# Attention scores with queries and keys as two fp16 parts on 64 rows, two heads side by side

## What is computed

```python
Q = proj(Wq, bq); K = proj(Wk, bk); V = proj(Wv, bv)        # (32, 2048, 16)
query_norms = jnp.linalg.norm(Q, axis=2)
_, top_idx = jax.lax.top_k(query_norms, top_u)              # top_u = 2048 // 5 = 409
Q_sel = jnp.take_along_axis(Q, top_idx[:, :, None], axis=1)
scores = jnp.einsum('bud,bld->bul', Q_sel, K) * scale
attn = jax.nn.softmax(scores, axis=-1)
out_sel = jnp.einsum('bul,bld->bud', attn, V)
out_full = jnp.zeros((BH, L, hd), dtype=x.dtype)
out_full = out_full.at[jnp.arange(BH)[:, None], top_idx].set(out_sel)
```

## Time and profile before

| | us |
|---|---|
| runs, median of 3 | 1194.58 (1193.07 to 1196.31) |
| profiled execution, its span | 1193.6 |
| PE busy | 993.4 (83%) |
| DVE busy | 904.4 (76%) |
| ACT busy | 646.3 (54%) |
| POOL busy | 713.0 (60%) |

### The profile page before, as it was taken

One profiled execution on the slowest core, in us unless ns is written; L12 is line 12 of the kernel. 1 busy time (PEld: TensorE's weight loads), 2 busy tenths in 40 slices (PEclk: granted clock), 3 DMA queues, 4 the chain that ended last, 5 costly groups with the idle time before them and its releaser, 6 DMA issues. The chain is left out here.

```text
span 1193.6 us, 29414 instructions
## 1 busy us (share of the span) xinstructions
PE 993.4 (83%) x7725; PEld 611.1 (51%) x7726; DVE 904.4 (76%) x2197; ACT 646.3 (54%) x1448; POOL 713.0 (60%) x840
## 2 busy tenths in 40 slices
PE   7999101399999999999977873299999999999995
PEld 4444000233333333333324662287778888888894
DVE  4895588778888888888866887667778777777774
ACT  2777185157777777777763441355454444444441
POOL 1687482447888888888659992124445544554443
PEclk9999655569999999999997895599999999999998
DMA  6244772201111111111306991399982322322332
GB/s 229 105 143 164 234 243 79 59 19 44 39 47 34 46 34 46 34 46 34 84 21 205 259 272 41 77 235 226 218 204 50 50 43 48 53 44 44 53 45 27
DMA packets 129229, 118.70 MB, mean 99 GB/s; under 512 B 18128, under 2 KB 117136, under 8 KB 129168
## 3 DMA queue, kind: packets, MB, share of 16 engines
q1 hardware_dynamic: 106904, 95.02, 27.0%
q0 software_dynamic: 20480, 21.53, 11.1%
q10 hardware_dynamic: 1784, 1.44, 0.4%
HBM read 57.27 MB, written 37.60 MB: 79 GB/s over the span
## 5 line engine op out<-in xcount | busy, mean ns | idle before, releaser
L994 DVE TENSOR_REDUCE attend_mxh<-attend_p_a 128x1 f32<-128x512 f32 x416 | 264.1, 685 | 56.9 <-PE attend_p_a L1137 52.0
L1076 ACT ACTIVATE w<-attend_p_b 128x409 f32<-128x409 f32 x480 | 228.8, 514 | 95.1 <-PE attend_p_b L1153 89.3
L1875 ACT ACTIVATE expert_hr<-expert_p,b1t 128x256 f32<-128x256 f32 (+1 forms) x376 | 134.3, 423 | 194.1 <-PE expert_p L1813 174.1
L1768 POOL DMA_INDIRECT out_x<-expert_ys,expert_drop x72 | 121.2, 1684 | 193.6 <-DVE expert_ys L1910 138.2
L1153 PE MATMUL attend_p_b<-attend_qt,w 98*128 98x409 bf16 x480 | 164.4, 347 | 0.3 <-ACT w L1076 0.3
L1137 PE MATMUL attend_p_a<-w,attend_qt 96*128 96x512 bf16 x384 | 151.0, 397 | 1.8 <-DVE attend_mxh L994 0.9
L1835 PE MATMUL expert_p<-w,expert_hhi 128*128 x800 | 136.7, 273 | 0.5 <-DVE expert_ys L1910 0.2
L1813 PE MATMUL expert_p<-expert_xhi,w 128*128 128x256 f16 x800 | 136.3, 273 | 0.0
L1758 POOL DMA_INDIRECT expert_xs<-h_d,expert_take x72 | 73.0, 1014 | 75.4 <-DVE expert_take L1914 54.4
L906 POOL DMA_INDIRECT attend_qsel<-q_d,idx x96 | 92.9, 967 | 39.8 <-POOL attend_idle L934 19.4
L1163 PE MATMUL attend_p_o<-w,attend_vh 128*32 128x409 f32 x1024 | 115.2, 522 | 1.1 <-ACT w L1076 0.6
(11 more groups left out here) (355 smaller groups left out, 1984.4 us busy)
## 6 DMA issues: line engine op xcount, KB each, us to landing
expert_wu<-w SPq DMA_DIRECT2D x88, 256.0 KB
w<-in_L_ffn_w SPq DMA_DIRECT2D x20, 512.0 KB, 4.5
q_d<-project_q SPq DMA_DIRECT2D x32, 256.0 KB, 3.1
w<-k_d SPq DMA_DIRECT2D x32, 192.0 KB
k_d<-project_k SPq DMA_DIRECT2D x45, 128.0 KB
x<-in_L_attn_x SPq DMA_DIRECT2D x8, 512.0 KB
attn_d<-zero SPq DMA_DIRECT2D x8, 512.0 KB
w<-k_d SPq DMA_DIRECT2D x32, 128.0 KB
```

Source lines behind the costliest of these rows:

```text
L994: dve.tensor_reduce(mxh[:, c, k:k + 1], chunk_bank(a)[:, :], AX, ALU.max).then_inc(a_done, 1)
L1076: act.activation(prob[:, j, :], tile_bank(j)[:, 0:TOP], ACT.Exp, scale=SCALE).then_inc(prob_done, 1)
L1768: pool.indirect_dma_start(out=out, out_offset=bass.IndirectOffsetOnAxis(ap=drop[u][:, s:s + 1], axis=0), in_=ys[u][:, s, :], in_offset=Non ...
L1875: last = act.activation(hr[g % 2][:, f, rows], p_1[g][:, f, rows], ACT.Relu, bias=cst["b1t"][:, bass.ds(e[s] * FB + 2 * g + f, 1)], scale= ...
```

## The change

Q and K become two fp16 parts each, scaled by 16. A score takes three products of parts: on 64 rows per head lie K high, K low, a gap of 16 rows, and K high again against Q high, Q high, the gap and Q low. In the gap the keys hold the constant 256, and the queries hold zeros for the chunks and minus the maximum / 256 in two parts for the tiles. Two heads then fill the 128 rows: head 2p on rows 0 to 63, head 2p+1 on rows 64 to 127, each product addressed to its half of PE (`tile_position=(64 * h, 0)`). So the unit of the block is a pair of heads, of which there are 16, all written out.

- Chunks and tiles of the two heads stand next to each other on PE; their number per head, 13 and 16, and their widths are as before. Chunks now have four banks, tiles three; the bank that held `p_m` is gone.
- The maximum is folded into the queries on PE: `turn_m` turns the queries a second time and adds the maximum in PSUM (24 products a pair), and ACT copies the whole. `turn_max` and its two-row copy are gone.
- `values` takes two tiles of two heads at a time, `results` gives both heads in one product of 34 columns, `minus_maximum` and `finish` treat both heads in one go.
- POOL's idle memsets are gone; gathers and scatters wait for DVE's count of maxima, two maxima a step. `vh` has two buffers of a pair, gathered queries three.
- Keys load by two DMAs of 32 and 16 rows per head. [...]
- In `project_block` the third parts go (POOL and ACT), and the last keys take one step of DVE instead of three steps.
- In `route_block` seven scatters are left over instead of four, and SP waits for them at tile 12.

```diff
-TERMS = 6
-PARTS = 3
+PARTS = 2
 HELD = 4
-STACK_K = ((0, 3), (3, 2), (5, 1))
-KR = TERMS * HD
+ROWS_H = HELD * HD
+UNIT = 16.0
...
-                        pool.tensor_tensor(krest[oc][:, :], yk[oc][:, :], k3[j % 2][oc][:, 0, :], ALU.subtract).then_inc(krest_done, 1)
-                def third_k(j):
-                    for oc in range(KD if j < NB - 1 else 0):
-                        pool.wait_ge(kpart1_done, KD * j + oc + 1)
-                        pool.tensor_tensor(k3[j % 2][oc][:, 2, :], krest[oc][:, :], k3[j % 2][oc][:, 1, :], ALU.subtract).then_inc(kpart2_done, 1)
-                unrolled([None, None, None, None, None, second, third, last_of_block(second_k), None, last_of_block(third_k)])
+                        pool.tensor_tensor(k3[j % 2][oc][:, 1, :], yk[oc][:, :], k3[j % 2][oc][:, 0, :], ALU.subtract).then_inc(kpart1_done, 1)
...
+                    j = NB - 1
                     dve.wait_ge(k_ps, KD * NB)
-                    dve.wait_ge(krest_done, KD * (NB - 1))
-                    dve.tensor_scalar(yk[1][:, :], p_k[1][:, :], bkb[:, 1, B - 1:B], None, ALU.add).then_inc(last_y[1], 1)
...
+                        dve.scalar_tensor_tensor(out=k3[j % 2][oc][:, 1, :], in0=p_k[oc][:, :], scalar=bkb[:, oc, B - 1:B], in1=k3[j % 2][oc][:, 0, :],
+                                                 op0=ALU.add, op1=ALU.subtract).then_inc(last_second, 1)
...
+        p_a = [ps(f"p_a{i}", [P, 512], F32) for i in range(4)]
...
+        def chunk_use(q, a, h):
+            return 1 + USES_A * q + 2 * a + h + (1 if a >= TURN_AT else 0)
...
+        def tile_use(p, j, h):
+            return 1 + USES_B * p + 2 * j + h + (1 if j == TPB - 1 else 0)
...
+            q, at = divmod(before - 1, USES_A)
+            if at < 2 * TURN_AT:
+                pe.wait_ge(a_done, CHP * q + at + 1)
+            elif at > 2 * TURN_AT:
+                pe.wait_ge(a_done, CHP * q + at)
...
+                def load_rows(p, h):
+                    sp.dma_start(kt[p % KB][HP * h:HP * h + 32, :], io["k3_d"][2 * p + h].rearrange("r d l -> (r d) l")).then_inc(k_here[p % KB], 16)
+                def load_again(p, h):
+                    sp.dma_start(kt[p % KB][HP * h + 48:HP * h + 64, :], io["k3_d"][2 * p + h, 0]).then_inc(k_here[p % KB], 16)
...
+                    if p + QB < NP:
+                        pool.wait_ge(mq_ps, p + 1)
+                        for i in range(2 * FULL):
+                            turn(p, at)
+                            gather_chunk(p + QB, i)
+                            at += 1
+                    if 1 <= p and p + 1 < NP:
+                        spread_v(p + 1)
+                    if p % 2 and (p + 3) // 2 < GN:
+                        turn(p, at)
+                        gather_tails((p + 3) // 2)
+                        at += 1
+                    if p > 0:
+                        pool.wait_ge(out_done, p)
+                        for i in range(2 * FULL):
+                            turn(p, at)
+                            scatter_chunk(p - 1, i)
+                            at += 1
+                    if p % 2 == 0 and p > 0:
+                        turn(p, at)
...
+                    dve.tensor_reduce(mxh[:, h, c, k:k + 1], p_a[chunk_use(q, a, h) % 4][:, :], AX, ALU.max).then_inc(a_done, 1)
...
+                for p in range(KB):
+                    for h in range(2):
+                        dve.memset(kt[p][HP * h + 32:HP * h + 64, :], STEP_M).then_inc(fill_done, 1)
+                    if p == 0:
+                        dve.memset(mxh[:, :, :, :], -3e38).then_inc(zero_done, 1)
+                        dve.memset(mpart[:, :, :, :], 0.0).then_inc(zero_done, 1)
+                for u in range(2):
+                    dve.memset(vh[u][:, :, :, W1:VC], 0.0)
+                    dve.memset(vh[u][:, :, :, HD], 1.0)
...
+                    maxima(p + 1, 3)
+                    if p > 0:
+                        finish(p - 1)
+                    for a in range(4, NA):
+                        maxima(p + 1, a)
+                    if p + 1 < NP:
+                        minus_maximum(p + 1)
+                    for a in range(3):
+                        maxima(p + 2, a)
+                    if p == NP - 1:
+                        for i in range(EARLY):
+                            split_weight(i)
...
+                def turned(q, into, low):
+                    last = None
+                    for c in range(QT):
+                        cols = slice(c * P, min((c + 1) * P, TOP))
+                        for h in range(2):
+                            n = 2 * q + h
+                            tail = slice(32 * (n % GH), 32 * (n % GH) + QTAIL)
+                            for r in range(2):
+                                w = 2 * h + r
+                                source = qsel[q % QB][:, h, c, 32 * r:32 * r + 32] if c < FULL else qtail[n // GH % 2][:, 32 * r:32 * r + 32]
+                                last = pe.matmul(into[32 * w:32 * w + 32, cols], source, cst["identb"][:, :] if c < FULL else cst["identb"][:, tail],
+                                                 start=True, stop=not (low and r), tile_position=(0, 32 * w))
+                                if low and r:
+                                    k = P if c < FULL else QTAIL
+                                    last = pe.matmul(into[32 * w:32 * w + 32, cols], mpart[0:k, h, c, :], cst["identb"][0:k, 0:k],
+                                                     start=False, stop=True, tile_position=(0, 32 * w))
+                    return last
...
+                        use = chunk_use(q, a, h)
+                        wait_chunk_bank(pe, use)
+                        into, rows = p_a[use % 4], slice(HP * h, HP * h + HP)
+                        if c < FULL:
+                            last = pe.matmul(into[:, :], qa[q % 2][rows, c * P:(c + 1) * P], kt[q % KB][rows, k * CH:(k + 1) * CH], start=True, stop=True, tile_position=(HP * h, 0))
+                        else:
...
+                        use = tile_use(p, j, h)
+                        wait_tile_bank(pe, use)
+                        rows = slice(HP * h, HP * h + HP)
+                        pe.matmul(p_b[use % 3][:, 0:TOP], kt[p % KB][rows, j * P:(j + 1) * P], qb[p % 2][rows, 0:TOP],
+                                  start=True, stop=True, tile_position=(HP * h, 0)).then_inc(b_ps, 1)
...
+                            w, j = 2 * h + i, 2 * b + i
+                            last = pe.matmul(p_o[32 * w:32 * w + VC, 0:TOP], vh[p % 2][:, j, h, :], prob[:, 2 * (j % (TPB // 2)) + h, :],
+                                             start=(b == 0), stop=(b == BLOCKS - 1), tile_position=(0, 32 * w))
...
+                for p in range(NP):
+                    scores_tile(p, 0)
+                    if p > 0:
+                        values(p - 1, 7)
+                    scores_tile(p, 1)
+                    scores_chunk(p + 1, 3)
+                    scores_tile(p, 2)
+                    if p > 0:
+                        results(p - 1)
+                    scores_tile(p, 3)
+                    scores_chunk(p + 1, 4)
+                    scores_chunk(p + 1, 5)
+                    scores_tile(p, 4)
+                    values(p, 0)
+                    scores_chunk(p + 1, 6)
+                    scores_tile(p, 5)
+                    values(p, 1)
+                    scores_tile(p, 6)
+                    scores_chunk(p + 1, 7)
+                    values(p, 2)
+                    scores_tile(p, 7)
+                    scores_chunk(p + 1, 8)
+                    turn_q(p + 2)
...
-                LATE = 8
+                LATE = 12
 
                 def load(t, c):
                     wait(sp, at_ps, t - 3)
-                    if isinstance(t, int) and t == LATE:
-                        sp.wait_ge(scattered, 16 * QT)
+                    if t == LATE if isinstance(t, int) else c == LATE % 4:
+                        sp.wait_ge(scattered, 16 * LAST)
...
+                    g, u = GN - 1, (N // 2 - 1) % 2
+                    h, c = divmod(i, QT - 1)
+                    rows, at = (cst["otail"][:, g, :], cst["tidx"][:, g:g + 1]) if i == LAST - 1 else (cst["outs"][u][:, h, c, :], cst["idx"][:, N - 2 + h, c:c + 1])
                     pool.indirect_dma_start(out=io["attn_d"], out_offset=bass.IndirectOffsetOnAxis(ap=at, axis=0), in_=rows, in_offset=None).then_inc(scattered, 16)
...
-                    if isinstance(t, int) and t < QT:
+                    if isinstance(t, int) and t < LAST:
```

More of the change, by code:

```diff
@@ L864, in steps, with turn_use @@
-        def steps(eng, run):
-            for c in range(U):
-                run(c, c)
-            with eng.Fori(1, N // U - 1) as i:
-                for c in range(U):
-                    run(U * i + c, c)
-            for c in range(U):
-                run(N - U + c, c)
-        def has(n):
-            return not isinstance(n, int) or 0 <= n < N
+        def chunk_use(q, a, h):
```

(60 more changed lines are left out.)

545 lines of the change are left out of this document (239 added, 306 removed).

## The result

The changed kernel took 1130.72 us (median of 4 runs, 1130.18 to 1131.14) beside 1193.82 for the kernel before on the same chip: a ratio of 0.9472, 95% interval 0.9459 to 0.9486. The forecast was 1137.5. The profiled execution spans 1128.4 us, 65.2 less than before.

A forecast was written before the change was run, and what follows sets the result against it. PE was taken to bound the attention, with DVE next at 18.8 us a pair. The span 1193.6 - 61.9 (attention) + 4.8 (routing) = 1136.5, plus 1.0 for the median, gave 1137.5 us; range 1116 to 1168.

The forecast's parts named there:

- rival 1: Attention: the two halves take turns, PE stays the bound at 21.7 us a pair; 1181 us (1165 to 1195), chance 0.11.
- rival 4: Attention: changing halves empties PE, 31 us a pair, 1324 us; a falling clock 1290; chance 0.04 for drained halves or clock.
- DVE takes over: Attention: DVE has 17.65 us of work a pair, PE 16.5; with waits a pair takes 18.8 (17.65 to 20.6).
- the wait at `finish`: Attention: DVE reaches `finish` at m + 4.9, m ending minus-maximum; results come at m + 5.65; stall 0.75 us a pair.
- the tight stretch: Attention, chunk 5 to chunk 8: PE needs 4.3 us against 3.6 of maxima, 0.6 to 0.75 buffered; 0.4 added.
- Two signs: Attention: DVE was to be busy above 93% and PE below 90%.
- Rival 3, POOL: Attention: POOL becomes the bound with indirect DMAs of 1.42 us, a pair 23.5, kernel slower at 1208 us; chance 0.03.
- Rival 2, no stall at all: Attention: DVE never stalls, 17.65 us a pair, 1120 us (1105 to 1122); chance 0.07.
- Projection: End of the projection, behind PE's last product: gain 5.4 us (2 to 6); POOL's and ACT's dropped third parts gain nothing.
- Fills: Start of the attention: eight fills take 14.6 to 17.9 us and delay the first maximum by 6.2.
- End of the attention: Last `finish` ends at 561.8 us instead of 623.7: -61.9.
- The clock, rival 4's second half: Attention: PE's clock falls while PE waits for DVE, 29 us a pair, 1290 us; chance 0.04 for drained halves or clock.

The follow-up runs named there:

- experiment 1: Changed kernel with every score product over all 128 rows, the other head's rows zero, so halves cannot work side by side: 1169.39 us, ratio 0.9786 to the kernel before.
- 4: Changed kernel with two more DVE reductions of 128x512 per pair of heads, on data always there: 1154.80 us, ratio 0.9662 to the kernel before.
- Experiment 7: Changed kernel with PE making six of the sixteen pairs of tiles twice: 1135.89 us, ratio 0.9494 to the kernel before.
- 5: Changed kernel with `finish` two maxima later on DVE and chunk 4 ahead of tile 2 on PE: 1135.38 us, ratio 0.9482 to the kernel before.
- 12: Changed kernel with `results` ahead of tile 2 on PE and four of the eight fills on ACT: 1122.77 us, ratio 0.9386 to the kernel before.
- experiment 11: Changed kernel with an ACT copy of 128x256 per tile put back in the projection: 1206.95 us, ratio 1.0075 to the kernel before.
- experiments 9 to 11: Changed kernel on one chip: `results` ahead of tile 2, 1204.80 us; that with four fills on ACT, 1203.34; an ACT copy per projection tile instead, 1206.95.
- 9: Changed kernel with `results` ahead of tile 2 on PE: 1204.80 us, ratio 1.0054 to the kernel before.
- 2: Changed kernel with `finish` two maxima later on DVE, PE's order unchanged: 1167.79 us, ratio 0.9779 to the kernel before.

## Why the prediction was right, step by step

- **What bounds.** PE was the bound, its score products were it, and halves side by side cost like one: 0.18 and 0.22 where I took 0.20 and 0.24 (experiment 1). Halves in turn, rival 1, would have cost 37 us; a change of halves that empties PE, rival 4, does not occur at all. The Trainium skill (TensorE: Matmul & The Clock Gate, Part 3: Packing small matmuls) has row groups run concurrently; the rows agree, with 0.36 / 0.18 = 2.0 for two halves.
- **DVE takes over** (17.65 a pair of work): right, by experiments 4 and 7. The period was 18.89 for 18.8. Within it, the wait at `finish` was 0.56 for 0.75 (results at m + 5.94, not 5.65, but DVE was there only at m + 5.4, since one chunk was 0.20 late and the six maxima before it took 3.85 for 3.7). The rest was 0.7 for the 0.4 that I had added for the tight stretch: that late chunk, those maxima, and `finish`, which takes 0.89 from its reciprocal to the next maximum (407.72 to 408.61) for 0.75.
- **Two signs were missed** by a little: DVE busy above 93% (92.3), PE below 90% (93.3). I took PE's busy share for its work. A tile's record is 0.35 long where the next product starts after 0.18, so short waits vanish under the records; only 1.2 us of idle time a pair are left (14.4 in twelve pairs). Experiment 7 measures what PE had in hand: of 1.1 us more work 0.25 reached the period.
- **Rival 3, POOL**, is out: POOL was busy for 167.73 of 260 us, its indirect DMAs took 0.97 on average, and it waited for maxima (280 to 540 us):

```profile
POOL attend_qsel L913 <- DVE attend_mxh L988: 28.5, 34, 1.5
```

- **Rival 2, no stall at all**, priced at 17 us, was mis-priced: the stall is part of a ring. `finish` waits for `results`, `values` waits for `finish`, and the next chunks wait for `values`. Taking 0.56 out at one place gave 0.1 (5) or 0.24 (12).
- **Projection**, the term that was most off: 5.4 forecast, 8.9 at the first fill. I held that the parts which leave POOL and ACT lie beside PE for nothing. PE's projection became 2.55 shorter, and one copy put back on ACT brings 1.84 of that back (experiment 11). The other 0.7 is the size of one stop for ACT's `ht`, 1.31 before, 0.29 in the changed kernel and 0.59 in 11; no run tests it. The tail behind PE was also shorter, by some 0.2 to the issue of the DMAs and by the DMAs themselves, 2.01 instead of 2.7.
- **Fills**: 7.9 for 6.2 (first maximum 19.2 us after the first fill, 11.3 before). Each of the eight cost 1.76 + 0.48, the upper of my two bounds. First exponential 252.8 for 256.2, by the projection.
- **End of the attention**: -67.4 for -61.9; 3.4 of the difference was there at the first exponential. The other 2.1 lie in the last two pairs and in the cold start, where PE ran at half clock for some 7 us behind the first exponential instead of 10 (granted clock 0.76 from 253 to 268: 15 x 0.24 / 0.5); the period of 18.89 for 18.8 took 1.2 off over thirteen pairs.
- **Routing**: 5.3 for 4.8. Not foreseen: 1.7 us less between the last `finish` and the routing. POOL's last scatter of the attention is now issued at 549.53, well before the last `finish`, and was at 621.31, inside the last head, before; that this is the reason is not tested.
- **The clock, rival 4's second half**, did not come in the changed kernel, but I took its 0.04 for remoteness, and it is near: in 5, whose stops on PE are at most 0.40 (0.37 in the changed kernel), the clock fell in three pairs of thirteen. That the changed kernel escaped it was not worked out beforehand, so this part of the hit is luck.

Left open: why the attention took some 24 us a pair in experiments 9 to 11, on one of the four chips of the experiments (the chip and the moment are not told apart). Experiment 11 has the attention of the changed kernel, so that kernel itself would have been expected at about 1200 there; it was not run on that chip. The kernel before was not touched (1197.5). Before, the attention looped over its heads, now it is written out; from 250 to 540 us the queues of kind "instruction" moved 34 packets (21 and 13) in the changed kernel and 14 (6 and 8) before. That the stops come from fetching instructions fits these numbers and DVE's and ACT's standing still together, but the packets themselves took no longer there (17 packets at 0.4% of the engines' time in 9, 21 at 0.5% in the changed kernel), so it is argued and not shown.

## What to carry to other kernels

Where products use at most half of the array's rows, place two independent ones on the two halves, next to each other in the list; then look for the engine that comes next, since most of the PE time won can't be spent. Before moving a step on a waiting engine, write down what stands ahead and behind on the engine that it waits for: in a ring of waits, a stall at one place is only worth what the next place can give. Keep an engine that clears or fills memory off the one that must start first, and count the operations of an engine that is not the bound as costly while its outputs feed the bound.

## What the runs showed of the hardware that I had not expected

- How little it takes to lose PE's clock, and that the length of a stop does not decide it. With stops of at most 0.37 us in its steady pairs the changed kernel stayed at the upper level, 2.4 GHz, from 280 to 540 us (1.00), and so did 12 with stops of up to 0.48. With 0.20 or 0.31 before `values`, and none over 0.40 (5), the clock fell to 1.2 GHz for parts of three pairs of thirteen (0.98 over the stretch), with 1.35 there (2) in ten of thirteen (0.90), with 1.38 before a chunk (4) in five of twelve (0.96). The same stops stand in pairs that kept the clock, so what decides is open.
- One kernel, two chips: 1203.34 and 1122.77 us, the kernel before 1197.47 and 1196.95 beside it. A ratio measured in one comparison need not hold in another; whether it was the chip or the moment is not shown.
- ACT fills 32 rows of 2048 fp16 in 1.9 us (7.70 for four), about DVE's 1.76, and without DVE's 0.48 between them.
